# One program instead of two phases: the FP4 feed-forward network starts inside the MLP's last round, and one key projection changes its step

## The reference, cut to what matters

```python
x = x + cross_attention(layernorm(x), ctx, wq, bq, wk, bk, wv, bv, wo, bo)   # 16 heads of 32, 2048 keys
x = x + performer_block(layernorm(x), ln1, wq, wk, wv, wo, ln2, w1, b1, w2, b2)  # its MLP: 512 -> 2048 -> 512, GELU
def fp4_linear(a, w):      # both are rounded to a grid of 8 magnitudes, in blocks of 16 with a scale each
    return einsum('bsk,nk->bsn', fp4(a), fp4(w))
y = layernorm(x)
h = silu(fp4_linear(y, w_gate)) * fp4_linear(y, w_up)      # 512 -> 1408
x = x + fp4_linear(h, w_down)                              # 1408 -> 512
```

## Time and profile before

| | before |
|---|---|
| median of three runs | 3635.07 us |
| the profiled execution's own time | 3638.49 us |
| its span in the trace | 3636.7 us |
| PE busy | 3483.4 us (96%) |
| DVE busy | 1790.2 us (49%) |
| ACT busy | 1107.3 us (30%) |
| POOL busy | 2034.2 us (56%) |
| moved by DMA | 174.67 MB, mean 48 GB/s |

### The profile page before, as it was taken

The page is one execution under the profiler, slowest core; times in us unless marked ns, Lnnn a source line. Parts: engine busy times, 40 slices in busy tenths (PEclk is TensorE's granted clock), DMA queues, the critical chain, the costliest instruction groups (busy, mean ns, idle before and its releaser), DMA issues. The chain is left out here.

```text
span 3636.7 us, 77830 instructions
## 1 busy us (share of the span) xinstructions
PE 3483.4 (96%) x31956; PEld 2685.8 (74%) x31956; DVE 1790.2 (49%) x3434; ACT 1107.3 (30%) x1264; POOL 2034.2 (56%) x1174
## 2 busy tenths in 40 slices
PE   7999999999999999999999999969998899869999
PEld 5777777777777777777777777757776788758887
DVE  5323233233233332332333323377887766679997
ACT  2233333333333333333333333341112322221111
POOL 2276876877878768768686787514444300023332
PEclk9999999999999999999999999999999999989999
DMA  3211011110110111101101011020113322130000
GB/s 122 71 39 45 25 45 33 36 33 27 44 43 25 45 33 36 37 24 52 35 28 42 33 36 45 4 103 33 55 46 120 122 80 79 56 108 24 17 23 18
DMA packets 83512, 174.67 MB, mean 48 GB/s; under 512 B 7200, under 2 KB 43296, under 8 KB 74016
## 3 DMA queue, kind: packets, MB, share of 16 engines
q1 hardware_dynamic: 82656, 168.20, 13.5%
q10 hardware_dynamic: 576, 2.10, 0.2%
HBM read 136.46 MB, written 33.82 MB: 47 GB/s over the span
## 5 line engine op out<-in xcount | busy, mean ns | idle before, releaser
L1039 DVE TENSOR_REDUCE x_maxima<-a_bank 128x1 f32<-128x512 f32 x960 | 593.2, 682 | 1236.7 <-PE a_bank L1163 1236.7
L92 PE MATMUL a_bank<-x_wv,x_ctx 128*128 128x512 f32 x3072 | 744.6, 397 | 2.5 <-DVE x_maxima L1033 2.5
L92 PE MATMUL a_bank<-x_ctx,x_wk 128*128 128x512 f32 x3072 | 741.7, 396 | 1.3 <-POOL x_ctx L900 1.3
L813 POOL TENSOR_TENSOR x_pairs<-x_probsT 128x1024 f32<-128x1024 f32 x240 | 572.2, 2384 | 238.8 <-ACT x_probsT L968 234.4
L92 PEld LDWEIGHTS a_bank<-x_wv,x_ctx 128*128 128x128 f32 x3072 | 564.4, 188 | 172.8 <-DVE x_maxima L1039 42.2
L92 PEld LDWEIGHTS a_bank<-x_ctx,x_wk 128*128 128x128 f32 x3072 | 564.8, 188 | 142.4 <-issue 19.3
L968 ACT ACTIVATE x_probsT<-a_bank 128x2048 f32<-128x2048 f32 x256 | 481.7, 1882 | 362.3 <-PE a_bank L1177 297.9
L962 ACT ACTIVATE x_v<-a_bank 128x512 f32<-128x512 f32 x256 | 153.0, 598 | 608.3 <-PE a_bank L92 608.3
L958 ACT ACTIVATE x_k<-a_bank,x_bk 128x512 f32<-128x512 f32 x256 | 176.2, 688 | 505.9 <-PE a_bank L92 505.9
L900 POOL TENSOR_TENSOR x_ctx<-x_ctx_raw,x_ctx 128x2048 fp32r<-128x2048 f32 x64 | 296.0, 4626 | 5.0
L1163 PE MATMUL a_bank<-x_k,x_q_max 32*128 32x512 f32 x2048 | 283.5, 633 | 12.8 <-ACT x_k L958 12.8
(11 more groups left out here) (201 smaller groups left out, 3884.0 us busy)
## 6 DMA issues: line engine op xcount, KB each, us to landing
x_ctx_raw<-in_ctx SPq DMA_DIRECT2D x64, 1024.0 KB, 4.9
m_ff_src<-in_w_ff SPq DMA_DIRECT2D x44, 192.0 KB, 2.5
wq_ff<-m_ff_dst SPq DMA_DIRECT2D x44, 192.0 KB, 1.9
m_w_raw<-in_w SPq DMA_DIRECT2D x32, 256.0 KB, 2.9
q_x<-in_x SPq DMA_DIRECT2D x16, 256.0 KB, 4.1
q_all<-q_out SPq DMA_DIRECT2D x16, 256.0 KB, 2.2
x_q_max<-q_all SPq DMA_DIRECT2D x16, 256.0 KB, 6.5
x_q<-q_all SPq DMA_DIRECT2D x16, 256.0 KB, 2.7
```

Source lines behind the costliest of these rows:

```text
L92: mm = pe.matmul(out, lhs[a], rhs[b], start=first and n == 0, stop=last and n == 2)
L813: eng.tensor_tensor(pairs[:], probsT[:, s % 2, :, 0:2], probsT[:, s % 2, :, 2:4], ALU.add).then_inc(paired, 1)
L1039: dve.tensor_reduce(maxima[:, c, g * HG + j:g * HG + j + 1], banks[:, j], AX.X, ALU.max).then_inc(maxed, 1)
```

## The change

Three things are changed.

1. **The batch loop.** The key projection of step 3 moves to step 4, which then has three items: key, value, value, in banks 5, 6 and 0. Step 3 has none. The wait ahead of `top` in step 4 now asks for the item of step 2.
2. **The MLP's schedule of weight pieces.** Of the 44 pieces 11 are rounded in round 0, 13 each in rounds 1 and 2, and 7 in round 3, there in every second step. `wq_ff` and the weights' source are laid out piece by piece.
3. **The feed-forward network.** `ffn_phase` becomes `ffn_stage` within the first block, with fixed places in SBUF and many semaphores of the first stage used again. Its 22 gate and up pieces are loaded, transposed and split during steps 1 to 12 of the MLP's last round (`tensor_step`, `vector_step`, `sync_step`), through banks 0 and 7. The first input tile is prepared in steps 12 to 15. The 12 pieces of the down weights are transposed between the gate and up projections of tile 0.

```diff
-    ITEM_BANKS = (5, 0)
+    ITEM_BANKS = ((), (5,), (5, 0), (5, 6, 0))
     LAST_BANKS = (5, 6, 0)
 
     def items(s):
 
         if s < DC:
-            return [("k", 0, s)]
+            return [("k", 0, s)] if s < DC - 1 else []
         c, half = divmod(s - DC, DC)
         if half < 2:
-            return [("v", c, 2 * half), ("v", c, 2 * half + 1)]
-        return [("k", c + 1, 2 * half - 4), ("k", c + 1, 2 * half - 3)]
+            todo = [("v", c, 2 * half), ("v", c, 2 * half + 1)]
+        else:
+            todo = [("k", c + 1, 2 * half - 4), ("k", c + 1, 2 * half - 3)]
+        return [("k", 0, DC - 1)] + todo if s == DC else todo
+
+    def placed(s):
+
+        todo = items(s)
+        return list(zip(todo, ITEM_BANKS[len(todo)]))
...
+        late.after.after = ffn_stage(nc, sc, bank, late.after, q, x2, wq_ff, out, id_t)
...
-                    before, todo = items(s - 1) if s else [], items(s)
+                    before = placed(s - 1) if s else []
                     if s >= DC:
 
                         pe.wait_ge(gathered, START + i * NS + (s - 1))
-                        await_item(n, *before[0])
+                        for it, b in before if s > DC else placed(s - 2):
+                            if b >= HG:
+                                await_item(n, *it)
                         if s > DC:
                             await_maxed(n, s - DC - 1)
                         top(n, s - DC, tops)
...
-                    for it, b in zip(items(s), ITEM_BANKS):
+                    for it, b in placed(s):
...
-                    if s >= DC:
-                        await_maxed(n, s - DC, 2)
-                    elif s:
-                        await_item(n, *before[0])
-                    else:
-                        await_item(i, "v", NKC - 1, TPC - 1)
-                    item(n, *todo[0], ITEM_BANKS[0])
-                    if len(todo) > 1:
-                        pe.wait_ge(exped, START + i * NS + (s + 1))
-                        item(n, *todo[1], ITEM_BANKS[1])
+                    for it, b in placed(s):
+                        if b < HG:
+                            pe.wait_ge(exped, START + i * NS + (s + 1))
+                        elif s >= DC:
+                            await_maxed(n, s - DC, b - HG + 1)
+                        elif s:
+                            await_item(n, *before[0][0])
+                        else:
+                            await_item(i, "v", NKC - 1, TPC - 1)
+                        item(n, *it, b)
...
-QPER = QPIECES // (B // MT)
+QPER = 13
...
+    FIRST_FF, LAST_FF = QPER - 2, QPIECES - 3 * QPER + 2
+    ff_v, ffq_v = ((a[0:FIRST_FF], a[FIRST_FF:FIRST_FF + 2 * QPER].rearrange("(m q) p n -> m q p n", q=QPER),
+                    a[FIRST_FF + 2 * QPER:]) for a in (w_ff, wq_ff))
...
+    def store_ff(sp, m, n, first=False, last=False):
+        sp.wait_ge(ff_ready, START + ff_pieces(m) + n + 1)
+        sp.dma_start(ff_at(ffq_v, m, n, first, last), ff_dst[:, n % 2]).then_inc(ff_stored[n % 2], 16)
...
-                if 2 <= f < QPER:
+                if first and 2 <= f < FIRST_FF:
+                    load_ff(sp, 0, f, first=True)
+                if not first and not last and 2 <= f < QPER:
                     load_ff(sp, m, f)
+                if last and f % 2 == 1 and f // 2 + 2 < LAST_FF:
+                    load_ff(sp, m, f // 2 + 2, last=True)
...
+                if first and 1 <= f <= FIRST_FF:
+                    store_ff(sp, 0, f - 1, first=True)
+                if not first and not last and 1 <= f <= QPER:
+                    store_ff(sp, m, f - 1)
+                if last and f % 2 == 1 and f // 2 < LAST_FF:
+                    store_ff(sp, m, f // 2, last=True)
+                if last:
+                    stage.after.sync_step(sp, f)
...
-                if f < QPER and not (first and f == 0):
-                    quantise_piece(dve, m, f - 1 if first else f)
-                if first and f == QPER:
-                    quantise_piece(dve, m, QPER - 1)
+                if first and 1 <= f <= FIRST_FF:
+                    quantise_piece(dve, m, f - 1)
+                if not first and not last and f < QPER:
+                    quantise_piece(dve, m, f)
+                if last and f % 2 == 0 and f // 2 < LAST_FF:
+                    quantise_piece(dve, m, f // 2)
+                if last:
+                    stage.after.vector_step(dve, f)
...
                 output(pe, m, f - 1, first)
+                if last:
+                    stage.after.tensor_step(pe, f)
...
+    g_t, u_t = ([[sc.at(f"f_{name}{n}_{k}", [P, DC, CHUNKS[n][1]], F32R, kb) for k, kb in enumerate(kbs)]
+                 for n, kbs in enumerate(places)]
+                for name, places in (("g", ((139, 147), (163, 171), (9, 17))), ("u", ((131, 155), (179, 1), (25, 33)))))
+    d_t = sc.at("f_d", [P, FC, 2, D], F32R, 41)
+    w_in = [sc.at(f"f_w_in{n}", [P, D], F32, 187 + 2 * ((n + 2) % 4)) for n in range(4)]
+    d_in = [sc.at(f"f_d_in{n}", [P, FF], F32, kb) for n, kb in enumerate((125, 199))]
...
+    bank = [banks[:, k] for k in (1, 4, 7, 0, 2, 3, 6, 5)]
+    w_bank, d_bank = [banks[:, 0], banks[:, 7]], [banks[:, 2], banks[:, 3]]
+
+    w_flat = wq_ff.rearrange("n p k -> (n p k)")
+    pieces = [(k, c0 + i * P, [a[n][j][:, :, i * P:(i + 1) * P] for j in range(2)])
+              for n, (c0, m) in enumerate(CHUNKS) for k, a in enumerate((g_t, u_t)) for i in range(m // P)]
+    d_pieces = [(r, c // P, m // P) for r in (1, 0, 3, 2) for c, m in CHUNKS]
+    steps = {f: range(2 * f - 2, 2 * f) for f in range(1, 10)}
+    steps.update({10: (18,), 11: (19, 20), 12: (21,)})
...
+    def load_weights(sp, n):
+        if n == 0:
+            sp.wait_ge(before.turned, START + B)
+            for k in range(2):
+                sp.wait_ge(before.ff_stored[k], START + 16 * before.ff_stores(NQ - 1, k))
+        if n >= 4:
+            sp.wait_ge(w_turned, C0 + n - 3)
+        k, t, dst = pieces[n]
+        first = (k * FF + t) * D
+        sp.dma_start(w_in[n % 4][:], w_flat[first:first + P * D].rearrange("(p n) -> p n", n=D))\
+            .then_inc(w_loaded[n % 4], 16)
+    def load_down(sp, r):
+        if r < 2:
+            for k in range(2):
+                sp.wait_ge(before.ff_stored[k], START + 16 * before.ff_stores(NQ, k))
+        else:
+            sp.wait_ge(w_turned, C0 + WP + (3 if r == 3 else 6))
+        first = 2 * FF * D + r * P * FF
+        sp.dma_start(d_in[r % 2][:], w_flat[first:first + P * FF].rearrange("(p n) -> p n", n=FF))\
+            .then_inc(w_loaded[r % 2], 16)
+    def load_first_x(sp, k):
+        sp.wait_ge(w_turned, C0 + min(19 + k, WP))
+        if k == 0:
+            sp.wait_ge(before.stored, START + 16)
+        load_x(sp, Tile(0, k))
+    def sync_step(sp, f):
+        if f == 0:
+            for n in range(4):
+                load_weights(sp, n)
+        for n in steps.get(f, ()):
+            if n + 4 < WP:
+                load_weights(sp, n + 4)
+        if f in (11, 12):
+            load_first_x(sp, f - 11)
+        if f == 13:
+            load_first_x(sp, 2)
+            load_first_x(sp, 3)
+        if f == FT - 1:
+            sp.wait_ge(before.gelu_done, START + NQ * FT)
+            sp.wait_ge(before.rb_ready, START + B)
+            load_down(sp, 1)
+            sp.wait_ge(before.acc_done, START + B)
+            load_down(sp, 0)
...
+        load_down(sp, 3)
+        load_down(sp, 2)
+        sp.wait_ge(before.stored, START + 16 * NQ)
...
+    def vector_step(dve, f):
+        for n in steps.get(f, ()):
+            weights_lo(dve, n)
+        if f == 12:
+            input_stats(dve, Tile(0, 0))
+        if f == 13:
+            input_scales(dve, Tile(0, 0))
+        if f == 14:
+            input_grid(dve, Tile(0, 0))
+        if f == FT - 1:
+            input_lo(dve, Tile(0, 0), w_bank[0])
...
+                if second(s):
+                    for n in range(4 * g, 4 * g + 4):
+                        down_lo(dve, n)
...
+    def turn_weights(pe, n):
+        pe.wait_ge(w_loaded[n % 4], loads_until(n))
+        await_from(pe, w_lo, W0, n - 1)
+        for c in range(DC):
+            mm = pe.transpose(w_bank[n % 2][:, c * P:(c + 1) * P], w_in[n % 4][:, c * P:(c + 1) * P], id_t[:])
+        mm.then_inc(w_turned, 1)
+    def turn_down(pe, n):
+        r, c, count = d_pieces[n]
+        pe.wait_ge(w_loaded[r % 2], d_loads_until(r))
+        pe.wait_ge(w_lo, W0 + WP + max(n - 1, 0))
+        for i in range(count):
+            mm = pe.transpose(d_bank[n % 2][:, i * P:(i + 1) * P], d_in[r % 2][:, (c + i) * P:(c + i + 1) * P], id_t[:])
+        mm.then_inc(w_turned, 1)
...
+    def tensor_step(pe, f):
+        for n in steps.get(f, ()):
+            turn_weights(pe, n)
+        if f == FT - 1:
+            pe.wait_ge(w_lo, W0 + WP)
+            turn_input(pe, Tile(0, 0), w_bank[0])
...
+                        if second(s) and done is up:
+                            if g == 0:
```

(8 more changed lines are left out.)

572 lines of the change are left out of this document (303 added, 269 removed).

## The result

| | before | after |
|---|---|---|
| median of the runs | 3635.30 us (4 runs) | 3594.15 us (4 runs, 3590.64 to 3596.26) |
| ratio after/before, 95% interval | | 0.9884 [0.9867, 0.9901] |
| the profiled execution's own time | 3638.49 us | 3596.26 us |
| its span | 3636.7 us | 3594.4 us |
| PE busy | 3483.4 us (96%) | 3472.0 us (97%) |

Forecast were 3590.6 us and a range of 3581 to 3605. The time lies in the range and 3.6 us above the value. But the terms of the sum are off by more than that, and they cancel: the batch loop, the last round and the passage together are 6.7 us short of the forecast, and the tiles, for which nothing was forecast, give 6.6 us.

The account below looks back on a forecast made before the run. PE was taken to bound the kernel, with time to win where it waits. Batch loop -8.7, last round +10.2 and passage -46.0 gave -44.5 us, from 3635.07 to 3590.6 us; range 3581 to 3605.

Parts of the forecast that it names:

- Batch loop, -8.7: Batch loop, step 4: gather's wait plus a third item cost 3.29 us instead of 3.87, 0.58 us less in 15 turns.
- a semaphore's way to PE is about 0.13 us: Batch loop, ahead of `top` in step 4: PE goes on about 0.13 us after DVE's gather ends.
- Pieces in the last round, 7.9 + 0.4: MLP's last round: 20 pieces at 0.79 us per two cost 7.9 us, transposing the first input tile 0.4 us.
- Start of the last round, +1.9: MLP's last round: first weight loads land behind the result's store, so `output(1)` begins 1.9 us later; bounds 0 to +3.5.
- then 0.4 us of transposes and 2.73 us of `hidden(2)`: Start of the MLP's last round: PE's work between the loads' landing at 3093.0 and `output(1)` at 3096.1 us.
- Passage, -46.0 (tile 1 at T + 31.4): From the MLP's last matmul (T) to tile 1: 31.4 us instead of 77.4, set by DVE's work and waits.
- From tile 1 on nothing is changed: Feed-forward tiles from tile 1: a steady tile stays at 24.69 us, no gain or loss.
- (a): Batch loop gains nothing, a wait for POOL replacing the removed one: 3599.3 us; chance 0.14.
- (c): Better: shorter gather wait, loads pass the store, tile 1 28 us after the MLP's last matmul: 3582.3 us; chance 0.12.
- (d): Tile 0 still waits at the MLP's end for POOL and the input's scales: 3602 us; chance 0.04.
- (b): DVE and loads bind more: bank waits in the last round, tile 1 at T + 38: 3602 us; chance 0.17.
- (e): Slower: TensorE's clock falls as transposes and waits mix into the last round: 3651 us; chance 0.03.

Follow-up runs that it names:

- wait_order: Changed kernel with step 4's wait for DVE's gather put last, on the first matmul of `top`, and one key-projection wait left out: 3590.27 us, ratio 0.9881.
- input_first: Changed kernel with the second input tile transposed, copied and halved ahead of the last two down-weight pieces in tile 0's step: 3588.77 us, ratio 0.9865.
- late_moves: Changed kernel with the last round's first four weight loads issued before its wait, and two 1-MB transfers moved from its start to step 4: 3588.46 us, ratio 0.9868.
- two_shifts: Changed kernel with f_hT 32 bytes higher and the low half of up's second chunk 128 bytes lower: 3596.56 us, run once.
- moving_only: Changed kernel with the down weights alone placed 128 bytes lower, f_hT untouched: 3597.53 us, run once.
- early_loads: Changed kernel with the last round's first four weight loads issued ahead of the wait for the third round's outputs and its result's store: 3595.30 us, ratio 0.9883.

## Why the prediction was right, and where it wasn't

- **Batch loop, -8.7: measured -5.2** (-5.0 alone). The mechanism is right: the wait for ACT went, that for the gather came, three items cost 2.72 us more. The step that failed is "a semaphore's way to PE is about 0.13 us": with three waits in a row it was 0.34 us. I had seen this order in the queues and priced it like a single wait. That is 2.7 to 3.0 of the missing 3.5 us, by wait_order.
- **Pieces in the last round, 7.9 + 0.4: measured about 9.1 + 0.5.** A steady step with two pieces takes 6.34 us, one without 5.44 (`hidden` from 3167.58 to 3173.02): 0.90 for two, not 0.79, since the 12 matmuls behind transposes take longer too (3099.41 to 3102.26, 2.85 us for 2.72). Sixteen pieces in steps 2 to 9, one in 10, two in 11 and one in 12 make 9 such pairs and 2 singles of 0.48.
- **Start of the last round, +1.9: measured +4.8.** `output(1)` began 17.9 us after the round's start, before 13.1. The loads behind the store came as foreseen: PE began at 3089.65, 11.67 us after the round's start; the forecast's two landings put it at 3093.0 - 3081.05 = 11.95. The step that failed is "then 0.4 us of transposes and 2.73 us of `hidden(2)`": it left out the clock, which was at its lower level behind this wait. Transposes and `hidden(2)` took 3.1 us longer than forecast. Against that, `output(1)` is now at the full clock, where before it took 4.61 us. 9.1 + 0.5 + 4.8 - 1.7 = 12.7 us, the window says 12.5. The Trainium skill, DMA: Bandwidth & Descriptors, section "Queues, rings and completion order", has each DMA engine take its descriptors in ring order; the two placements of the loads (3.35 us of waiting behind the store, none ahead of it) agree.
- **Passage, -46.0 (tile 1 at T + 31.4): measured -45.1 (T + 32.3).** Right in mechanism and size; DVE was what it waited for, and input_first showed it by moving the input's work forward in the queues.
- **"From tile 1 on nothing is changed": wrong by -6.6 us.** This was an error, and a lucky one. The three terms above fall short of the forecast by 3.5, 2.3 and 0.9 us, 6.7 in all, and this one gives 6.6 back. Without it the median would have been about 3601 us: still in the range, but 10 us above the value. New places of the buffers were part of the diff and I gave them no thought.
- **Rivals.** (a), (c) and (d) did not occur. (b) did not either: PE waited for no bank in the round, and tile 1 began at T + 32.3; only the loads bound, at the round's start. (e) did not: the clock fell only at the waits. What the prediction cites beside (e) from the Trainium skill, TensorE: Matmul & The Clock Gate, section "Part 4: PE-mode transpose", that transposes don't engage the full clock, finds no support here: late_moves has 1.00 over the whole round, though there transposes take only 0.8 of the 6.3 us of a step, and rows 10, with transposes alone, have 0.92.

## What to carry to other kernels

When a stage is moved into another block, its buffers get new addresses; compare their starts in bytes before calling the rest of it unchanged. Put the wait that is fulfilled last on the instruction that needs it, behind the others. Large transfers that nobody needs soon should be issued late: here they held up the loads behind them, an engine's own instructions went on only when they had thinned out, and what they released on GpSimd slowed VectorE just where TensorE waited for it. And a wait that is removed shows the next one: measure what else was late behind it.

## What the runs showed of the hardware that I had not expected

- **Operand addresses.** A matmul of 512 columns starts every 227 ns with both operands at multiples of 256 bytes (after), every 231 to 235 ns with the stationary one 32 bytes off (two_shifts), and 232.5 ns in the mean with the moving one 128 bytes off (moving_only). For 384 columns before and after show no difference (173 ns). Other offsets of one operand alone were not tried.
- **An engine can stop for its code, and longer while the DMA engines are full of data.** DVE stood still for 4.58, 4.19 and 1.00 us (after, early_loads, late_moves) and went on 1.76, 1.77 and 1.78 us after an 8-KB piece of instructions had begun to move. In the kernel before it stood still for 1.61 us until 2429.69, 1.76 us after such a piece. That the pieces belong to DVE is read from these times; that the data ahead of them made the first two late is read from late_moves. The Trainium skill, Runtime: NRT & Kernel Launch, section "Instruction fetch mechanics", says that fetching the next block is mostly hidden, but that a taken branch outside the blocks held must wait for a DMA. Here the stop came shortly after the loop over rounds had ended; that the branch is the cause was not tested.
- **VectorE beside GpSimd.** While GpSimd added the bias (5.5 us in early_loads), a VectorE instruction that takes 0.36 us took 1.31; in the kernel before, a low half of 0.69 us took 1.75. No run moved this addition alone.
